# First expert stage of a two-layer decoder: the shared expert first, started group by group, and the choice of experts in pieces

## The reference

```python
probs = jax.nn.softmax(xf @ w_router, axis=-1)           # 8 experts
top_vals, top_idx = jax.lax.top_k(probs, TOP_K)          # TOP_K = 2
gates = top_vals / jnp.sum(top_vals, axis=-1, keepdims=True)
cw = jnp.einsum('tk,tke->te', gates, onehot)
h1 = jnp.einsum('td,edh->eth', xf, w1)                   # hidden width 256
h3 = jnp.einsum('td,edh->eth', xf, w3)
y = jnp.einsum('eth,ehd->etd', jax.nn.silu(h1) * h3, w2)
out = jnp.einsum('etd,te->td', y, cw)
out = out + jax.nn.silu(xf @ sw1) * (xf @ sw3) @ sw2     # the shared expert: no gate
```

## Time and profile before

| what | us |
| --- | --- |
| time, median of three runs | 1146.97 |
| the three runs | 1144.10, 1147.93, 1146.97 |
| the profiled execution, its own time | 1145.01 |
| its span (first to last instruction) | 1143.3 |
| the stage: from the last `add_attended` to the last down of the 36 rounds | 330 to 508 of the span |

### The profile page before, as it was taken

One profiled execution on the slowest core, in us unless ns is written; L12 is line 12 of the kernel. 1 busy time (PEld: TensorE's weight loads), 2 busy tenths in 40 slices (PEclk: granted clock), 3 DMA queues, 4 the chain that ended last, 5 costly groups with the idle time before them and its releaser, 6 DMA issues.

```text
span 1143.3 us, 15921 instructions
## 1 busy us (share of the span) xinstructions
PE 986.6 (86%) x5754; PEld 734.3 (64%) x5754; DVE 864.4 (76%) x1840; ACT 534.4 (47%) x904; POOL 409.1 (36%) x448
## 2 busy tenths in 40 slices
PE   6666767677979999989779999889986899999998
PEld 4222323232768888876338888857665779999997
DVE  6689999998666555572868888868996478788886
ACT  6664646464543222236800000055663657767774
POOL 6188989898210010121742222253441001001110
PEclk9978989899979999998975555679999899999999
DMA  6000000000000010200000000000000000000001
GB/s 170 0 0 0 1 1 1 0 0 1 1 1 15 15 28 16 64 1 1 0 0 1 1 1 1 1 1 2 2 2 1 1 1 19 20 19 19 20 19 38
DMA packets 19865, 13.87 MB, mean 12 GB/s; under 512 B 3067, under 2 KB 18313, under 8 KB 19786
## 3 DMA queue, kind: packets, MB, share of 16 engines
q1 hardware_dynamic: 19786, 12.84, 4.0%
HBM read 11.79 MB, written 1.05 MB: 11 GB/s over the span
## 4 chain that ended last, share of the span: by engine, by line
PE 52%; DVE 16%; ACT 4%; issue 2%; POOL 1%; DVEq 0%; ACTq 0%
PE ps L1067 18%; PE ps L1061 16%; PE ps L1268 6%; DVE small L945 2%; PE ps L1230 2%; PE ps L1370 2%; DVE lm L902 2%; DVE G L948 1%; DVE rrec L908 1%; PE ps L1312 1%; DVE G L912 1%; PE ps L1261 1%; DVE sdot L906 1%; DVE stats L656 1%; PE ps L1302 1%
## 5 line engine op out<-in xcount | busy, mean ns | idle before, releaser
L1067 PE MATMUL ps<-xhl,whl 128*128 128x512 f32 x960 | 251.0, 412 | 13.0 <-DVE xhl L673 6.7
L1067 PEld LDWEIGHTS ps<-xhl,whl 128*128 128x128 f32 x960 | 182.0, 196 | 53.1 <-issue 12.1
L1268 PE MATMUL ps<-lm,ones 128*128 128x16 f32 x504 | 127.0, 376 | 11.6 <-DVE lm L902 8.2
L1268 PEld LDWEIGHTS ps<-lm,ones 128*128 128x128 f32 x504 | 115.4, 318 | 24.6 <-DVE lm L902 18.8
L1061 PEld LDWEIGHTS ps<-R,G 128*128 128x128 f32 x1024 | 119.0, 192 | 6.4 <-DVE G L991 4.1
L1061 PE MATMUL ps<-R,G 128*128 128x128 f32 x1024 | 119.7, 275 | 3.1 <-DVE G L991 3.1
L628 ACT ACTIVATE G<-ps,w_exp_bi 128x512 f32<-128x512 f32 x128 | 90.0, 703 | 65.9 <-PE ps L1067 54.9
L424 ACT ACTIVATE LN<-X,stats,rstd 128x128 f32<-128x128 f32 x48 | 21.1, 488 | 207.8 <-POOL stats L271 207.6
L307 POOL TENSOR_TENSOR R<-G,R 128x1024 f32<-128x1024 f32 x43 | 104.6, 2449 | 25.3 <-ACT R L478 25.1
L1103 PE MATMUL ps<-bc,sel 96*128 96x512 bf16 x128 | 48.9, 412 | 71.7 <-DVE R L780 26.6
L763 DVE TENSOR_TENSOR_SCAN R<-ps,R 128x1024 f32<-128x1024 f32 x43 | 97.5, 2278 | 9.6 <-POOL R L316 4.8
(11 more groups left out here) (228 smaller groups left out, 1782.6 us busy)
## 6 DMA issues: line engine op xcount, KB each, us to landing
ew<-in_w_dram SPq DMA_DIRECT2D x24, 128.0 KB, 2.2
R<-in_exp_wi_dram SPq DMA_DIRECT2D x8, 256.0 KB, 2.8
R<-in_exp_wo_dram SPq DMA_DIRECT2D x8, 256.0 KB, 3.2
X<-in_x_dram SPq DMA_DIRECT2D x4, 256.0 KB, 4.3
out_dram<-X SPq DMA_DIRECT2D x4, 256.0 KB, 2.3
w_ctxT<-in_ctxT_dram SPq DMA_DIRECT2D x1, 487.5 KB
ew<-in_sw_dram SPq DMA_DIRECT2D x3, 128.0 KB, 2.2
w_W_in<-in_W_in_dram SPq DMA_DIRECT2D x1, 256.0 KB, 4.6
```

The costliest lines, as they stand in the source:

```text
L1067: ins = mm(out, whl[:, wslot(n), i, m * P:(m + 1) * P], xhl[:, j, gcols(g)], start=k == 0, stop=k == 2)
L1268: ins = mm(slot(0, t), ones[:], lm[:, t % 2, 1, h, :], start=False, stop=h == HI - 1, skip_group_check=True)
```

## The change

Three things are edited, and they hang together.

1. **The shared expert comes first.** SP loads `sw1`, `sw3`, `sw2` as number 0 and expert k - 1 as number k. Rounds 0 to 3 are then those of the shared expert, which need no choice.
2. **Round g starts when group g is normalized.** Norm 2 transposes into banks 4 to 7 instead of 0 to 3. PE transposes groups 0 and 1, waits until all attention outputs are read out of banks 0 to 3 (`pv_res`), and begins round 0; the transposes of group 2 follow in round 0, those of group 3 in round 1, all router matmuls together in round 2. ACT's copies and DVE's `ln_lower` of groups 2 and 3 move between the `Silu` and products of rounds 0 and 1.
3. **The choice is cut up**: subtracting the largest logit and clearing the diagonal in round 3 (with ACT's `Exp` behind its `Silu` of round 3), half of the comparisons in round 4, the other half and the sum in round 5, and the weights in round 6, where `add_gated(4)` and `add_gated(5)` follow one another.

```diff
-        ln_bank = lambda i, g: g + 4 * (i == 5)
+        ln_bank = lambda i, g: g + 4 * (i in (2, 5))
...
 # SP
+            for k in range(E + 1):
+                if k >= 2:
+                    sp.wait_ge(S["down0"], NG * (k - 1))
+                s = "w_e0b" if k % 2 else "w_e0a"
+                if k == 0:
+                    expert0(0, s, a["sw1"], a["sw3"], a["sw2"])
                 else:
-                    expert0(0, "w_e0a", a["sw1"], a["sw3"], a["sw2"])
+                    expert0(k % 2, s, a["w1"][k - 1], a["w3"][k - 1], a["w2"][k - 1])
...
 # ACT (silu_up(i) holds the two Silu of round i, unchanged)
-            layer_norm(2)
+            for g in range(NG):
+                normalize(2, g)
+                if 1 <= g < NG - 1:
+                    copy_xnT(2, g - 1)
+            for i in range((E + 1) * NG):
+                silu_up(i)
+                if i < 2:
+                    copy_xnT(2, NG - 2 + i)
-                if i == 1:
+                if i == 3:
                     act.wait_ge(S["rt_sub"], 1)
                     sc.activation(router[:, 1, :, :], router[:, 0, :, :], ACT.Exp).then_inc(S["rt_exp"], 1)
...
 # DVE (choose is cut into compare and weigh; the layer norm without ln_lower of groups 2 and 3)
+            def hidden(i):
+                if i >= 2:
+                    dve.wait_ge(S["down0"], i - 1)
+                for m in range(M0):
+                    dve.wait_ge(S["silu0"], M0 * i + m + 1)
+                    v.tensor_tensor(hidr[:, i % 2, m * GT:(m + 1) * GT], sh[:, i % 2, m * GT:(m + 1) * GT],
+                                    bank(2 + m)[:, 0, :], ALU.mult).then_inc(S["hid0"], 1)
+
+            def add_gated(i):
+                if i >= NG:
+                    dve.wait_ge(S["res0"], i - NG + 1)
+                add_expert(i, cw0, i // NG - 1 if i >= NG else E, "down0", "res0")
+
+            probs = router[:, 1]
             for i in range((E + 1) * NG + 1):
                 if i < (E + 1) * NG:
+                    hidden(i)
+                if 1 <= i != NG + 1:
+                    if i == NG + 2:
+                        weigh(probs, cw0[:, :, 0:E]).then_inc(S["rt_cw"], 1)
+                        dve.wait_ge(S["rt_cw"], 1)
+                        add_gated(NG)
+                    add_gated(i - 1)
+                if i < 2:
+                    ln_lower(2, NG - 2 + i)
+                elif i == NG - 1:
+                    subtract_top_logit()
+                elif i == NG:
+                    dve.wait_ge(S["rt_exp"], 1)
+                    compare(probs, range(E // 2))
+                elif i == NG + 1:
+                    compare(probs, range(E // 2, E))
+                    step(v.tensor_reduce(router[:, 2], pair[:, 0], AX.X, ALU.add))
...
 # PE
             transpose_xn(2, 0)
-            for g in range(NG):
-                if g + 1 < NG:
-                    transpose_xn(2, g + 1)
-                pe.wait_ge(S["ln_xnT"], 2 * NG + g + 1)
-                for b in range(g * GB, (g + 1) * GB):
-                    ins = mm(bank(7)[:, 0, b * E:(b + 1) * E], xnT[:, b * T:(b + 1) * T], w["router0"][:], start=True, stop=True)
-            ins.then_inc(S["rt_mm"], 1)
+            transpose_xn(2, 1)
+
+            def router_logits():
+                pe.wait_ge(S["ln_xnT"], 3 * NG)
+                pe.wait_ge(S["ln_lo"], 2 * NG - 1)
+                for b in range(B):
+                    ins = mm(bank(6)[:, 0, b * E:(b + 1) * E], xnT[:, b * T:(b + 1) * T], w["router0"][:], start=True, stop=True)
+                ins.then_inc(S["rt_mm"], 1)
+
+            pe.wait_ge(S["pv_res"], B)
             for i in range((E + 1) * NG + 1):
...
-                    if i == 0:
-                        pe.wait_ge(S["ln_lo"], 2 * NG)
+                    if e == 0:
+                        pe.wait_ge(S["ln_lo"], NG + g + 1)
...
+                if i < 2:
+                    transpose_xn(2, NG - 2 + i)
+                if i == 2:
+                    router_logits()
```

More of the change, by code:

```diff
@@ L537, in _, with silu_up @@
                                   accum_out=small[:, 2, g * GB + b:g * GB + b + 1]).then_inc(S["sc_exp"], 1)
-            layer_norm(2)
-            for i in range((E + 1) * NG):
+            def silu_up(i):
                 for m in range(M0):
@@ L687, in layer_norm, with compare @@
                         beside(g - 2)
-            def choose(val, cw):
-                v.memset(pair[:, 0].rearrange("p b e f -> p b (e f)")[:, :, 0:E * E:E + 1], 0.0)
-                for e in range(E):
+            def compare(val, experts):
+                for e in experts:
                     if e:
@@ L698, in choose, with weigh @@
                 step(ins)
-                step(v.tensor_reduce(router[:, 2], pair[:, 0], AX.X, ALU.add))
+            def weigh(val, cw):
                 step(v.tensor_scalar(router[:, 3], router[:, 2], 1.5, None, ALU.is_lt))
@@ L821, in add_attended, with subtract_top_logit @@
                 dve.wait_ge(S["pv_res"], GB * (g + 1))
-            layer_norm(2, add_attended)
-            def choose_experts():
+            for g in range(NG):
+                add_attended(g)
+                ln_stats(2, g)
+                if g >= 1:
+                    ln_norm(2, g - 1)
+                if g >= 2:
+                    ln_lower(2, g - 2)
+            ln_norm(2, NG - 1)
+            def subtract_top_logit():
                 dve.wait_ge(S["rt_mm"], 1)
-                lg = bank(7)[:, 0, 0:B * E].rearrange("p (b e) -> p b e", b=B)
+                lg = bank(6)[:, 0, 0:B * E].rearrange("p (b e) -> p b e", b=B)
                 step(v.tensor_reduce(small[:, 1, :], lg, AX.X, ALU.max))
@@ L830, in choose_experts @@
                     .then_inc(S["rt_sub"], 1)
-                dve.wait_ge(S["rt_exp"], 1)
-                choose(router[:, 1], cw0[:, :, 0:E]).then_inc(S["rt_cw"], 1)
-                dve.wait_ge(S["rt_cw"], 1)
+                v.memset(pair[:, 0].rearrange("p b e f -> p b (e f)")[:, :, 0:E * E:E + 1], 0.0)
             def add_expert(i, cw, e, dn, rs):
```

## The result

The changed kernel takes **1139.5 us** in the median of seven runs (1135.05 to 1142.24), against 1144.56 for the kernel before in its seven. The ratio is 0.9945, with a 95% interval of 0.9925 to 0.9964. Six more runs of the same kernel, taken later beside the experiments, gave 1137.37 and a ratio of 0.9938 (0.9922 to 0.9954), and one more gave 1135.66; the median of all fourteen is 1137.5. Forecast were 1138.7, a range of 1134.5 to 1142.5 and a gain of 7.3 us. The measured ratios are gains of 6.3 and 7.1 us on 1144.56; the plain difference of the two medians of seven is 5.1 us, and over all fourteen runs it is 7.1.

What follows compares the result with a forecast made beforehand. PE was taken to bound the kernel. Terms -8.45 + 1.0 + 3.5 - 2.04 - 1.9 + 0.6 gave -7.3 us, from 1146.0 to 1138.7 us, range 1134.5 to 1142.5.

Steps and rivals of the forecast that it cites:

- the sum: Added gains and costs from the first up to the up of round 4: -7.3 us, carried to the kernel's end.
- The bound: PE bounds the stage: 32 rounds of 4.52 us, 144.67 us together, which the change cannot shorten.
- Start of round 0: PE begins the first up at about 330.25 in place of 338.70, a gain of 8.45 us.
- Router: All 32 rows now between the ups, costing 3.5 us at the down's 0.111 each; bounds 3.2 and 6.4 us.
- The choice's wait and the second half-clock stretch: PE's wait before 355.40 and the slow clock behind it both go: -2.04 and -1.9 us.
- The clock at the start: Half clock for 5.5 us from the first up, costing 2.75 in place of 2.15: +0.6 us, bounds +0 and +1.5.
- the walk: Following each piece beside PE's work: nothing waits in round 0, by 0.5 us; with an earlier clock rise PE waits for ACT.
- ACT in round 3: Tightest place: Exp and table loads between the Silus of rounds 3 and 4 leave 0.4 us, costed at nothing.
- Rival A: An early stall in rounds 0 to 2 brings the clock down again; gain only 3.5 to 5 us; chance 0.17.
- rival C: Clock stays at half in first rounds mixed with transposes and narrow router; slower, some 75 us if through 36 rounds; chance 0.03.
- Rivals B: The early start yields nothing; only the choice's 3.9 us or half of it is gained, 1142 to 1146 us; chance 0.08.
- Rival D: Clock rises at once or router nears its lower bound; gain 9 us or more, under 1137 us; chance 0.07.

Runs made afterwards that it cites:

- router_twice: The changed kernel with each router matmul issued twice, 64 rows in one stretch; 1144.29 us, ratio 0.9999 to the kernel before.
- the second profile: The changed kernel itself, unaltered, profiled again as a control; median 1137.37 us over six runs, ratio 0.9938 to the kernel before, stretch 173.65 us.
- late_start: The changed kernel with norm, router and first up put back as before, keeping the shared expert first and the choice in pieces; 1139.94 us, ratio 0.9957.
- warm: The changed kernel plus nine unread 512-column matmuls in PE's idle time before the first up, which then runs at full clock; 1136.89 us, ratio 0.9941.
- third of the changed kernel: The changed kernel itself, unaltered, run once more for another profile; 1135.66 us, stretch 170.41 us.
- lump: The changed kernel with the whole choice in one piece behind the addition of round 4; 1140.62 us, ratio 0.9959 to the kernel before.
- router_split again: Second execution of the changed kernel with the router's matmuls in four pieces of 8 rows; 1141.03 us in one run, stretch 170.41 us.

## Why the prediction was right

- **The time and the gain.** The stage gained 7.1 us in the profile where the sum had 7.3, and that part is no luck. The time is in part luck: 1138.7 counts from 1146.0, while the kernel before has a median of 1144.56 in seven runs. From there the sum gives 1137.3, which is what all fourteen runs have (1137.5); the first seven lay higher, at 1139.5.
- **The bound.** PE through 32 rounds of 4.52 us, untouched: from the up of round 4 to the end of the last counted down, 353.21 to 497.86, are 144.65 us, as before.
- **Start of round 0**: PE begins 0.05 us behind DVE's last attention addition, as worked out. In the span it is 329.42, because what lies ahead happened to be 0.8 us shorter.
- **Transposes** 0.61 + 0.44 = 1.05 us for a forecast of 1.0.
- **Router** 3.47 us for 3.5 at full clock: the row of the down was the right neighbour (0.108 us against 0.111 a row), and the upper bound of 0.20 is what a row costs at half clock, as router_twice and the second profile show.
- **The choice's wait and the second half-clock stretch**, 3.9 us: late_start measures 4.3, of which 0.3 are a sooner rise of the clock at the start.
- **The clock at the start**: 5.5 us at half were forecast, and the rise came between 334.5 and 335.5, that is 5.1 to 6.1 us after the first up. `warm` shows that the size of this term is not what decides: with no half clock at all the stage is as long. The sum priced it as if each us counted; the walk, which saw PE wait for ACT after an early rise, was the better part of the text.
- **ACT in round 3**: a margin of 0.4 was forecast, 0.3 to 0.6 are there. By the drain that the Trainium skill adds to a table load ("ScalarE: Activation LUTs", "What ACT_TABLE_LOAD costs") PE would have waited; the `Silu` 0.01 us behind the load disagrees with it here too.
- **Rival A** was half right. No wait came back, but the clock did fall in the first rounds in one of the three profiles of the changed kernel, in the router. I had put the danger into a stall, and the narrow columns only into the slower rival C. The price was 3.3 us of the 7.1 in that execution.
- **Rivals B and C** didn't come. C's price was wrong, though: the 36 rounds are 36 x 4.52 = 163 us of PE at full clock, and an up takes 5.49 us at half clock for 2.74 at full, so half clock all through would have cost some 160 us and not 75. The 75 are about half of the time at full clock; a us that passes at half clock costs 0.5, but twice as many pass. Rival D, a gain of 9 or more through an early rise, didn't come either: `warm` shows that the early rise alone brings nothing, and the router took 3.47 us, above its lower bound of 3.2.

## What to carry to other kernels

A decision that only late work needs can go behind early work that doesn't need it, but in pieces that fit into the idle time of its engine in a round: in one piece it cost 2.5 us of wait and 1.8 us of clock again. Before paying to take a cost away, ask what lies parallel to it: the half clock of the first up was worth nothing until ACT's table load moved too, and both together, with the router in pieces, brought 2.6 us of the stage (167.76 against 170.38). Look at the granted clock behind a long row of narrow matmuls even where TensorE is never idle, and try them in pieces between wide ones: here 64 rows in a row cost 6.6 us of clock, and 32 cost 3.3 and 1.6 us in two profiles of six.

## What the hardware showed that I had not expected

- TensorE's clock fell to 1.2 GHz with PE busy without a gap in the profile, in the middle of a row of 8-column matmuls: at 347.2 in the second profile of the changed kernel, some 2.4 us into the router, and at 346.2 in router_twice, 2.3 us into it. It stayed there for 6.8 and 13.6 us. The Trainium skill, "TensorE: Matmul & The Clock Gate", section "HAM oscillation — how this bites in real kernels", tells of idle gaps as what brings the clock down; in these runs it came down without one.
- What lies behind the stage differs by as much as the change is worth, with the same code. From the first transpose of the next norm to the end it took 635.6 us before and in the first profile after, but 631.4, 635.2, 630.9 and 638.0 in others (second and third of the changed kernel, lump, router_split again). In the second profile of the changed kernel the stage was 3.3 us longer than in the first, what lies behind it 4.2 us shorter and what lies ahead of it 1.6 us longer, so the two times are almost the same (1137.94 and 1137.14). One place of it: in 738 to 774 the first profile of the changed kernel has a mean PEclk of 0.72, the second 0.86.

```profile
738.00:774.00 36.00, 31.11 (x224) 21.34 (x222) 21.41 (x28) 19.91 (x33) 19.06 (x35) 0.72 0.00 1
```

```profile
738.00:774.00 36.00, 31.17 (x247) 21.22 (x247) 25.41 (x48) 22.60 (x39) 20.34 (x37) 0.86 0.00 1
```

  This is why lump has a smaller span than the first profile of the changed kernel (1134.8 against 1135.4) with a stage that is 4.4 us longer. For a change of this size, compare the stage, or many runs; one execution's time against another's says little.
